# One-hots of an edge-matrix stage made in halves, and fewer table words read by TensorE's queue

## What is computed

```
h = relu(layernorm(x))
norm_h = h / max(norm(h), 1e-12)
p = softmax of (beta * edge_weight) over the edges of one source
L0 = (1 + eps) * h + segment_sum(norm_h[src] * p[:, None], dst)
x = x + L0
# layers 1 and 2 need, for each pair of nodes, how many edges join them and the sum of their
# weights: segment_sum(... [src], dst) becomes a product with these two matrices
```

## Time and profile before

| | us |
|---|---|
| time, median of 3 executions (6819.9 to 6832.18) | 6825.32 |
| the profiled execution: its own time | 6829.46 |
| its span | 6828.0 |
| TensorE matmul busy, whole span | 4951.0 (73%) |
| TensorE weight loads busy | 3093.0 (45%) |
| VectorE busy | 4675.9 (68%) |
| ScalarE busy | 1634.4 (24%) |
| GpSimd busy | 2614.4 (38%) |

### The profile page before, as it was taken

The page is one execution under the profiler, slowest core; times in us unless marked ns, Lnnn a source line. Parts: engine busy times, 40 slices in busy tenths (PEclk is TensorE's granted clock), DMA queues, the critical chain, the costliest instruction groups (busy, mean ns, idle before and its releaser), DMA issues. The chain is left out here.

```text
span 6828.0 us, 71514 instructions
## 1 busy us (share of the span) xinstructions
PE 4951.0 (73%) x19096; PEld 3093.0 (45%) x19096; DVE 4675.9 (68%) x6628; ACT 1634.4 (24%) x3088; POOL 2614.4 (38%) x2433
## 2 busy tenths in 40 slices
PE   2777774258888886997888897788868886555555
PEld 1255553235555554785333277333324443333333
DVE  7699999957777776798999989899981101111112
ACT  0044442023333200323455410355530003000000
POOL 0177777778888885000000000000000000777774
PEclk9999999999999998656999965899999998555555
DMA  2000002434343311453333356233326666222221
GB/s 78 7 8 8 8 8 58 113 107 135 124 133 128 109 43 35 141 159 101 113 114 111 106 155 186 89 113 113 112 76 241 241 241 165 53 53 53 53 53 45
DMA packets 427374, 681.15 MB, mean 100 GB/s; under 512 B 86757, under 2 KB 308611, under 8 KB 417355
## 3 DMA queue, kind: packets, MB, share of 16 engines
q1 hardware_dynamic: 349282, 569.41, 25.9%
q0 software_dynamic: 77808, 107.93, 6.4%
HBM read 536.29 MB, written 140.87 MB: 99 GB/s over the span
## 5 line engine op out<-in xcount | busy, mean ns | idle before, releaser
L1043 POOL DMA_INDIRECT ring<-rel_dram,rel_col x782 | 744.4, 952 | 3345.7 <-SPq L71 3107.6
L954 PE MATMUL total<-to,from 128*128 128x256 f32 x2816 | 857.6, 420 | 228.5 <-issue 140.8
L790 POOL DMA_INDIRECT cells_dram<-rec,place x816 | 830.1, 1017 | 451.9 <-issue 242.7
L1077 PE MATMUL total<-ring,onehot 128*128 x1612 | 541.5, 498 | 455.7 <-DMA ring<-rel_dram,rel_col 452.0
L1612 PE MATMUL sums<-acc,hw 128*64 128x400 f32 x2144 | 759.5, 510 | 140.2 <-DVE acc L1546 139.7
L848 POOL DMA_INDIRECT ring<-l_dram,src_pair x600 | 758.0, 1263 | 182.9 <-issue 182.9
L1054 DVE TENSOR_SCALAR onehot<-iota,loc_pair 128x128 f32<-128x128 f32 x806 | 177.2, 286 | 816.9 <-PE total L1077 816.9
L954 PEld LDWEIGHTS total<-to,from 128*128 128x128 f32 x2816 | 467.1, 195 | 573.0 <-issue 545.8
L1077 PEld LDWEIGHTS total<-ring,onehot 128*128 128x128 f32 x1612 | 402.8, 310 | 594.8 <-issue 532.7
L1612 PEld LDWEIGHTS sums<-acc,hw 128*64 128x64 f32 x2144 | 269.1, 138 | 596.0 <-issue 316.5
L545 PE MATMUL node<-moved,onehot 128*128 128x75 f32 x1584 | 365.8, 426 | 221.6 <-DVE moved L419 221.6
(11 more groups left out here) (389 smaller groups left out, 8038.8 us busy)
## 6 DMA issues: line engine op xcount, KB each, us to landing
count<-ac_dram SPq DMA_DIRECT2D x200, 800.0 KB, 4.3
strip<-ac_dram SPq DMA_DIRECT2D x75, 1600.0 KB, 7.1
ac_dram<-stage SPq DMA_DIRECT2D x125, 640.0 KB, 3.5
h<-ac_dram SPq DMA_DIRECT2D x26, 1600.0 KB, 8.0
acc<-ac_dram SPq DMA_DIRECT2D x24, 1600.0 KB, 8.4
lo_row<-lo_dram SPq DMA_DIRECT2D x102, 256.0 KB, 3.5
rel_dram<-rows SPq DMA_DIRECT2D x25, 1024.0 KB, 5.4
mask_dram<-mask SPq DMA_DIRECT2D x25, 800.0 KB, 5.0
```

What stands on the lines that cost most here:

```text
L790: pool.indirect_dma_start(m.cells_dram[:, :], bass.IndirectOffsetOnAxis(ap=m.place[:, j:j + 1], axis=0), m.rec[:, j, :], None, bounds_chec ...
L954: nc.tensor.matmul(spots[:, at(spot), :].rearrange("p o n -> p (o n)"), from_[:, n % 2, u, :], to[:, n % 2, u, :, :].rearrange("p k d -> p ...
L1043: pool.indirect_dma_start(ring[:, c % SLOTS, :], None, m.rel_dram[:, :], bass.IndirectOffsetOnAxis(ap=m.rel_col[:, c:c + 1], axis=0)).then ...
L1077: last = nc.tensor.matmul(total[:, at(col, D)], onehot[:, j % U, :], rows, start=False, stop=False, skip_group_check=True)
```

## The change

Four edits:

1. `mark` makes the one-hots of four chunks instead of eight (instructions over 512 elements), and VectorE does it as soon as the four chunks whose buffer half it takes are done. TensorE waits for `from_hot` and `to_hot` before each four chunks instead of each eight.
2. The segment number that TensorE awaits moves into bits 16 and up of the word in `spot_row`. `need_row` and its load go; the word is shifted to get the number. The bounds check that stood behind the load of `need_row` now stands behind that of `spot_row`.
3. The offsets of two groups share one word of `near_row`, so TensorE loads one for each second group.
4. The setup of the two tables is changed to match, by one instruction on rows of one partition each way.

```diff
@@ setup
+            step(v.scalar_tensor_tensor(near[:, 0::2], near[:, 1::2], 64.0, near[:, 0::2], ALU.mult, ALU.add))
+            step(v.tensor_copy(m.near_row[:, :], near[:, 0::2]))
@@ cells
+            step(v.tensor_scalar(seg, seg, 1.0, None, ALU.add))
+            step(v.scalar_tensor_tensor(word, seg[:, G - 1::G], float(SPOTS) ** G, word, ALU.mult, ALU.add))
             step(v.tensor_copy(m.spot_row[:, :], word))
-            step(v.tensor_scalar(seg, seg, 1.0, None, ALU.add))
-            step(v.tensor_copy(m.need_row[:, :], seg[:, G - 1::G]))
@@ dense_and_l0, VectorE
-            def mark(n):
-                b, cols = n % 2, slice(n * BB, (n + 1) * BB)
-                v.tensor_tensor(to[:, b, :, 1, :], mid(m.iota[:, :], BB), bc(rec[:, cols, 1], P), ALU.is_equal).then_inc(hot, 1)
...
+            def mark(k):
+                b, cols = k // 2 % 2, slice(k * G, (k + 1) * G)
+                half = slice(k % 2 * G, (k % 2 + 1) * G)
+                v.tensor_tensor(to[:, b, half, 1, :], mid(m.iota[:, :], G), bc(rec[:, cols, 1], P), ALU.is_equal).then_inc(hot, 1)
...
-                dve.wait_ge(summed, n * BB + BB)
-                if n + 2 < TURNS:
-                    mark(n + 2)
+                for k in (2 * n, 2 * n + 1):
+                    dve.wait_ge(summed, k * G + G)
+                    if n + 2 < TURNS:
+                        mark(k + 4)
@@ dense_and_l0, TensorE
             def word_of(k):
-                return pe.value_load(m.spot_row[0:1, k:k + 1])
-            def need_of(k):
-                return pe.value_load(m.need_row[0:1, k:k + 1], min_val=1, max_val=LAST)
+                return pe.value_load(m.spot_row[0:1, k:k + 1], min_val=SPOTS ** G, max_val=(LAST + 1) * SPOTS ** G - 1)
+            def need_of(word):
+                return pe.snap(word >> (4 * G), min_val=1, max_val=LAST)
...
-                pe.wait_ge(from_hot, n + 1)
-                pe.wait_ge(to_hot, n + 1)
                 for k in range(n * BB // G, (n + 1) * BB // G):
+                    pe.wait_ge(from_hot, k + 1)
+                    pe.wait_ge(to_hot, k + 1)
                     pe.wait_ge(freed, need)
...
-                            nears.append(pe.value_load(m.near_row[0:1, g:g + 1]))
+                            if g % 2 == 0:
+                                nears[g // 2] = pe.value_load(m.near_row[0:1, g // 2:g // 2 + 1])
```

More of the change, by code:

```diff
@@ L247, in _ @@
                 step(v.scalar_tensor_tensor(near[:, :], own[:, :], D * 4.0 ** k, near[:, :], ALU.mult, ALU.add))
-            step(v.tensor_copy(m.near_row[:, :], near[:, :]))
+            step(v.scalar_tensor_tensor(near[:, 0::2], near[:, 1::2], 64.0, near[:, 0::2], ALU.mult, ALU.add))
+            step(v.tensor_copy(m.near_row[:, :], near[:, 0::2]))
             step(v.tensor_scalar(own[:, :], tile_first[:, 0::G], float(D), None, ALU.mult))
@@ L882, in _ @@
             v = nc.vector
[L884 to L890 removed]
+            def mark(k):
+                b, cols = k // 2 % 2, slice(k * G, (k + 1) * G)
+                half = slice(k % 2 * G, (k % 2 + 1) * G)
+                v.tensor_tensor(to[:, b, half, 1, :], mid(m.iota[:, :], G), bc(rec[:, cols, 1], P), ALU.is_equal).then_inc(hot, 1)
+                v.tensor_tensor(from_[:, b, half, :], mid(m.iota[:, :], G), bc(rec[:, cols, 0], P), ALU.is_equal).then_inc(from_hot, 1)
+                dve.wait_ge(hot, k + 1)
+                v.tensor_tensor(to[:, b, half, 0, :], to[:, b, half, 1, :], bc(rec[:, cols, 2], P), ALU.mult).then_inc(to_hot, 1)
             def place(g):
@@ L918, in _ @@
             dve.wait_ge(rec_in, 16)
-            mark(0)
-            mark(1)
+            for k in range(4):
+                mark(k)
             for n in range(TURNS):
@@ L934, in word_of @@
             def word_of(k):
-                return pe.value_load(m.spot_row[0:1, k:k + 1])
-            def need_of(k):
-                return pe.value_load(m.need_row[0:1, k:k + 1], min_val=1, max_val=LAST)
+                return pe.value_load(m.spot_row[0:1, k:k + 1], min_val=SPOTS ** G, max_val=(LAST + 1) * SPOTS ** G - 1)
+            def need_of(word):
+                return pe.snap(word >> (4 * G), min_val=1, max_val=LAST)
+            nears = {}
             pe.wait_ge(cleared, 4)
-            word, need = word_of(0), need_of(0)
+            word = word_of(0)
+            need = need_of(word)
             for n in range(TURNS):
-                nears = []
-                pe.wait_ge(from_hot, n + 1)
-                pe.wait_ge(to_hot, n + 1)
                 for k in range(n * BB // G, (n + 1) * BB // G):
+                    pe.wait_ge(from_hot, k + 1)
+                    pe.wait_ge(to_hot, k + 1)
                     pe.wait_ge(freed, need)
@@ L958, in _ @@
                                 next_word = word_of(k + 1)
-                            if c == 1:
-                                next_need = need_of(k + 1)
+                            if c == G - 1:
+                                next_need = need_of(next_word)
                         if c == 2 and k % (BB // G) < len(groups_of[n]):
                             g = groups_of[n][k % (BB // G)]
-                            nears.append(pe.value_load(m.near_row[0:1, g:g + 1]))
+                            if g % 2 == 0:
+                                nears[g // 2] = pe.value_load(m.near_row[0:1, g // 2:g // 2 + 1])
                     word, need = next_word, next_need
-                for g, near in zip(groups_of[n], nears):
+                for g in groups_of[n]:
+                    near, low = nears[g // 2], 6 * (g % 2)
                     if g % PER_LOAD == 0:
@@ L975, in _ @@
                         if k:
-                            col = pe.snap((near >> (2 * k)) & (3 * D), min_val=0, max_val=3 * D)
+                            col = pe.snap((near >> (2 * k + low)) & (3 * D), min_val=0, max_val=3 * D)
                             out = window(g)[:, at(col, D)]
@@ L1864, in gnn_kernel @@
         with ExitStack() as tables:
-            m.spot_row, m.need_row, m.ends_row = (tables.enter_context(nc.sbuf_tensor(n, [1, k], I32)) for n, k in (
-                ("spot_row", NCH // G), ("need_row", NCH // G), ("ends_row", NT * SEGS)))
-            m.near_row, m.base_row = (tables.enter_context(nc.sbuf_tensor(n, [1, NPP // G], I32)) for n in ("near_row", "base_row"))
+            m.spot_row, m.ends_row = (tables.enter_context(nc.sbuf_tensor(n, [1, k], I32)) for n, k in (
+                ("spot_row", NCH // G), ("ends_row", NT * SEGS)))
+            m.near_row, m.base_row = (tables.enter_context(nc.sbuf_tensor(n, [1, k], I32)) for n, k in (
+                ("near_row", NPP // G // 2), ("base_row", NPP // G)))
             m.src_pair = tables.enter_context(nc.sbuf_tensor("src_pair", [P, NPP], I32))
```

## The result

Before: 6827.57 us, the median of 4 runs (6819.9 to 6832.18). Changed: 6714.31 us, the median of 4 (6708.88 to 6721.86). The ratio is 0.9837 (0.9822 to 0.9851), 113 us less; 128 less were predicted (6697 us). The profiled spans, 6828.0 and 6712.8 us, differ by 115.2.

A forecast was written before the change was run, and what follows sets the result against it. Two chains bound the stage: GpSimd's 1275 us and TensorE's queue. GpSimd's 127 us less, the smaller relief, plus about 1 us of tail gave -128: 6701, shown as 6697 us; range 6655 to 6775 (8 in 10).

The forecast's parts named there:

- GpSimd sets the end: Woven stage: GpSimd's gather chain, 1275 us before, still ends last after the change, with 127 us less.
- A gather waits for the end of a mark and takes 0.82 us from there: GpSimd's gathers: one started during a VectorE mark is held until that instruction ends, then runs 0.82 us by itself.
- 127 us less on GpSimd: GpSimd's gathers in the stage: with halved marks their delay falls from 254 to 127 us; bounds 43 to 184 less.
- 352 triples x 0.36: Gather delay left after the change: 0.36 us for each triple of VectorE's marks, 127 us in all.
- one catch a triple, released at the next end: GpSimd's gathers: each short mark triple holds one gather, released after 0.68 or 1.28 us; the next need falls outside.
- None near 2.0 us, the longest about 1.6: Sign in GpSimd's gathers after the change: no duration near 2.0 us, longest about 1.6; median still 0.95.
- rival 4: VectorE's two triples run back to back, every gather caught, three a turn: 63 us slower, 6888 us; chance 0.03.
- VectorE is hidden: VectorE's 1031 us of work stays hidden while the stage exceeds 1050 us; 293 us of idle time shrink to about 100.
- Rival 3: VectorE becomes the bound, at 0.68 us a mark start to start: gain only 40 to 80 us, 6745 to 6785; chance 0.08.
- TensorE's queue: 83 to 126 us less: TensorE's queue: 453 loads removed, 136 to 163 us, less 37 to 53 us for added shifts and waits.
- Two chains, the later one counts: Stage end is the later of GpSimd's chain, 127 us less, and TensorE's queue, 136 to 179 us earlier.
- Rivals 1 and 2: Gathers get no faster, 6825 us, chance 0.05; gathers outpace TensorE's queue, which then sets the end, 6650 to 6690, chance 0.10.

The follow-up runs named there:

- the kernel with the numbers in PSUM: Changed kernel, the marks' first two instructions reading 0 to 127 from PSUM, one PSUM window for the groups instead of two: 6833.96 us (one execution).
- the added waits: Kernel before, with TensorE waiting for the one-hots twice a turn, 176 instructions more on its queue: 6834.78 us, ratio 1.0007.
- the memsets: Kernel before, with three one-column memsets more a turn on VectorE behind the marks, 528 in all: 6827.32 us, ratio 0.9997.
- the late halves: Changed kernel, with VectorE waiting for all eight chunks of a turn before either half: 8411.61 us, 1.0431 of the kernel before on that chip.
- the mask: Changed kernel, bounds check behind the word's load replaced by a mask: 8340.13 and 8339.41 us, 1.0338 and 1.0341 of the kernel before on those chips.

## Why the prediction was right, point by point

**GpSimd sets the end.** Right: its gathers lost 116.1 us, the last add came 115.7 us earlier, and rows are still waited for at the end.

**A gather waits for the end of a mark and takes 0.82 us from there.** Right for the gathers that start between 0.04 us into a mark and 0.19 us before its end (194 of 194 in the changed kernel), and shown to need two inputs in SBUF (0 of 163 held with one in PSUM). It is not always the next end (below). The page SBUF — State Buffer of the Trainium skill (section "Who interferes with whom") says that a VectorE instruction with two SBUF inputs contends with GpSimd's reads; the kernel with the numbers in PSUM agrees (0.95 us with one input in PSUM, 1.42 with two in SBUF). The page's inference that such an instruction doesn't stall the making of descriptors is contradicted by the gathers of both kernels.

**127 us less on GpSimd.** The sum is near (116.1), its parts are not, and that it came out near is luck. The term "352 triples x 0.36" was mis-sized. Gathers that were released at the first end cost 47.0 us, 0.13 a triple, since only 208 gathers were held by a mark at all: of 458 that start while a mark runs, 250 run through. The rule "one catch a triple, released at the next end" failed at the word "released": 46 gathers were passed over at one to five ends, 88.9 us. "None near 2.0 us, the longest about 1.6" was therefore wrong, by 45 gathers and 2.5 us. It is rival 4's mechanism in a stronger form, triples back to back (85 of them), which the prediction saw only as many catches and not as a long one. The two errors nearly cancel (-80 and +88.9, with 3.6 under `place`).

Why so many run through can be read from the starts. Behind a held gather the next one starts 0.81 + 0.30 = 1.11 us behind the mark's end. With long marks that is 0.06 us into a later mark: 140 gathers of the kernel before started there, and all 140 were held, for nearly the whole mark. With marks of 0.69 us, 0.60 from start to start, it is three starts on, at the hand-over from one mark to the next: 89 gathers of the changed kernel started within 0.04 us of it, and none was held. The prediction had put them outside the triple. A few hundredths of a microsecond decide here, so the same halving need not give as much in another kernel.

**VectorE is hidden.** Right: 0.69 us a mark, 0.60 from start to start, and 121.9 us of waiting for TensorE left (under 150 forecast). Rival 3 is out.

**TensorE's queue: 83 to 126 us less.** Right. Its own time, from the first matmul to the last add less the waits for rows and ScalarE (the waits for marks, 66.6 and 66.4 us, stand in both), was 2694.49 - 1416.8 - 53.0 - 16.9 = 1207.8 us and is 2578.82 - 1416.2 - 41.5 - 26.0 = 1095.1, 112.7 less. That this comes from the queue edits follows from the halves with TensorE's program as it was, where the same sum gives 2.0 us. The queue edits alone were not timed on a chip where the kernel before takes 6830 us.

**Two chains, the later one counts.** Right. That the queue edits are needed is measured: halves with TensorE's program as it was give 62.6 us of the 113. That the halves are needed is argued, from GpSimd's 1275 us and from the added waits that cost next to nothing. Rivals 1 and 2 are out: the gathers got faster, and rows are still what TensorE waits for at the end.

**What stays open.** On two of three chips of these series TensorE's queue stands still in episodes, and with the halves and their waits there are more of them. The halves with TensorE's program as it was, the added waits and the memsets were meant to part the causes there, but ran on the first kind of chip. So what in the halves does it is not known; early marks (the late halves lose as much) and the bounds check (the mask saves only 51 us of 322) are not the whole of it. Nor is it shown whether avoiding the 46 missed ends would help: they cost GpSimd 88.9 us, but TensorE's queue has only the 41.5 us that it now waits, so my estimate is 41 us at most.

## What to carry to other kernels

Where two engines' chains both end near the stage's end, work out each alone: the smaller relief counts, and here the halves by themselves show little over half of what both parts give. Making VectorE's instructions with two SBUF inputs shorter can shorten what a gather waits, but where they follow one another without a pause a gather can miss several ends; look for gathers that span several, and at where in an instruction they start, not just at the mean. Time a change on more than one chip before it is kept: this one is 1.6% faster on one and 3.9% slower on another.

## What was not expected of the hardware

A gather that waits for VectorE's instruction to end can miss that end when the next instruction follows at once: 46 of 816, up to 4.075 us for one, where the longest before was 2.0. Short marks are not needed for it: with marks of eight chunks the longest gather took 3.2 us in the kernel with the added waits and 3.4 us in the one with the memsets, and on the other chips the queue edits alone have 24 and 23 over 2.2 us. And chips differ by more than the change: the same kernel takes about 6827 us on one, and 8064 and 8069 on two others. In every kernel profiled there the softmax over sources takes about 2029 us instead of 1040, and in the woven stage single register instructions of TensorE's queue that take 36 ns as a rule took about 0.7 us each, for stretches at a time.
